# Output projection's tiles at other slots, and its reciprocal root on another engine, in an attention layer with a feed-forward layer

## What is computed

```python
x = x + layernorm(attention(layernorm(x), Wqvk, Wo))   # 16 heads of 32, causal, softmax, then @ Wo
x = x + layernorm(ffn(layernorm(x), W1, b1, ..., W2, b2))
```

```python
wv = jnp.einsum('bsth,bthi->bshi', weights, v).reshape(b, s, d)
return wv @ Wo
```

## Time and profile before

| | us |
|---|---|
| median of 3 runs | 3446.77 (3444.99 to 3449.8) |
| profiled execution | 3445.31 |
| its span | 3443.5 |
| PE busy in the span | 3148.3 (91%) |
| DVE busy | 2237.1 (65%) |
| ACT busy | 2070.4 (60%) |
| POOL busy | 1327.9 (39%) |

### The profile page before, as it was taken

How to read it: one execution, slowest core, us unless ns; L and a number is a source line. 1 busy time by engine, 2 the same in 40 slices (tenths; PEclk the granted TensorE clock), 3 DMA queues, 4 the chain that set the end, 5 groups by cost and what they waited for, 6 DMA issues and landing times. The chain is left out here.

```text
span 3443.5 us, 76542 instructions
## 1 busy us (share of the span) xinstructions
PE 3148.3 (91%) x29476; PEld 1797.2 (52%) x29476; DVE 2237.1 (65%) x4207; ACT 2070.4 (60%) x2451; POOL 1327.9 (39%) x718
## 2 busy tenths in 40 slices
PE   7999898999898989989899858999999999999998
PEld 3444344766666666767676623444444444444443
DVE  5455555777676777767677624666666666666665
ACT  3222332988888887979797924555555555555554
POOL 2000000988888897979798930000000000000000
PEclk9999999999999999999999978999999999999999
DMA  6578783122222222222222132111111111111110
GB/s 181 171 218 248 232 260 90 52 70 82 58 84 64 81 69 78 63 84 58 86 66 79 44 101 90 37 38 39 37 37 37 37 37 37 37 37 37 37 37 25
DMA packets 328304, 279.95 MB, mean 81 GB/s; under 512 B 151056, under 2 KB 270032, under 8 KB 325968
## 3 DMA queue, kind: packets, MB, share of 16 engines
q1 hardware_dynamic: 328016, 275.82, 27.8%
HBM read 148.87 MB, written 92.80 MB: 70 GB/s over the span
## 5 line engine op out<-in xcount | busy, mean ns | idle before, releaser
L1257 POOL TENSOR_TENSOR a_prob_lo<-a_prob,a_prob_hi 128x2048 f16<-128x2048 f32 (+2 forms) x448 | 1191.9, 2689 | 185.8 <-ACT a_prob_hi L1168 184.2
L229 DVE TENSOR_REDUCE u_mx<-a_pw 128x4 f32<-128x512 f32 (+1 forms) x1178 | 730.6, 657 | 166.4 <-PE a_pw L215 126.6
L1158 ACT ACTIVATE a_prob<-a_pst,a_lift,w_exp_scale 128x1024 f32<-128x1024 f32 (+1 forms) x640 | 709.6, 1124 | 207.5 <-PE a_pst L1095 101.4
L1592 PE MATMUL f_ph<-f_xT,f_w 128*128 128x512 f16 x3072 | 707.5, 380 | 26.9 <-DMA f_xT<-f_xh 26.9
L1602 PE MATMUL f_py<-f_w,f_act 128*128 128x512 f16 x3072 | 707.6, 380 | 25.0 <-DVE f_work L1445 12.3
L1168 ACT ACTIVATE a_prob_hi<-a_prob 128x2048 f16<-128x2048 f32 (+2 forms) x448 | 583.3, 1302 | 0.0
L1559 ACT ACTIVATE f_hidden_work<-f_ph,w_turn,w_fold 128x512 f32<-128x512 f32 x256 | 199.3, 779 | 582.8 <-PE f_ph L1592 582.3
L1403 POOL TENSOR_TENSOR f_ve<-f_mv,f_eps 128x4 f32<-128x4 f32 x32 | 9.0, 283 | 1329.9 <-DVE f_mv L1427 1329.9
L1122 PE MATMUL a_acc<-u_vt,a_prob_hi 128*128 128x33 f16 x9216 | 466.0, 178 | 49.8 <-POOL a_prob_lo L1257 28.7
L1592 PEld LDWEIGHTS f_ph<-f_xT,f_w 128*128 128x128 f16 x3072 | 301.3, 98 | 392.2 <-issue 31.8
L1602 PEld LDWEIGHTS f_py<-f_w,f_act 128*128 128x128 f16 x3072 | 299.0, 98 | 395.4 <-issue 17.7
(11 more groups left out here) (161 smaller groups left out, 3345.7 us busy)
## 6 DMA issues: line engine op xcount, KB each, us to landing
qk_parts<-q_stage SPq DMA_DIRECT2D x128, 256.0 KB, 2.9
u_qp<-qk_parts SPq DMA_DIRECT2D x192, 128.0 KB, 2.7
u_kp<-qk_parts SPq DMA_DIRECT2D x192, 128.0 KB, 2.8
v_parts<-q_vstage SPq DMA_DIRECT2D x16, 1056.0 KB, 5.2
u_vt<-v_parts SPq DMA_DIRECT2D x32, 528.0 KB, 4.8
q_x<-in_L_attn_h_dram SPq DMA_DIRECT2D x16, 1024.0 KB, 8.6
q_raw<-in_L_ffn_W_dram SPq DMA_DIRECT2D x16, 1024.0 KB, 7.7
u_xr<-in_L_attn_h_dram SPq DMA_DIRECT2D x64, 256.0 KB, 3.1
```

The source lines that it names most:

```text
L229: dve.tensor_reduce(out, src[:, 0:n * len(heads)].rearrange("p (h n) -> p h n", n=n), AX_X, ALU.max).then_inc(units.released, 1)
L1158: act.activation(prob[:, k % PR, :, off:QC], pst[:, k % 2, :, off:QC], ACT.Exp, scale=exp_scale, bias=lift[:, :]).then_inc(exp_done, 1)
L1257: pool.tensor_tensor(prob_lo[:, first % HR:first % HR + steps, :, off:QC], prob[:, first % PR:first % PR + steps, :, off:QC], prob_hi[:, f ...
L1592: last = pe.matmul(ph[:, f % HB, :], w1s[:, a, k, f * P:(f + 1) * P], xT[:, e, b, k, :], start=(j == 0), stop=(j == len(terms) - 1))
```

## The change

The tiles of a set begin at slots 10, 18, 26, ... 66, counted from the batch's last unit: 10 and 18 of unit 3, 6 and 14 of the next unit 0, 2, 10 and 18 of unit 1, 6 of unit 2. Since the last tiles now read group 0 after the next batch has begun to write it, `oT` gets a fifth place, and group 0 uses the one or the other in turn. For this the place must be known by batch parity, so the loop of six turns of one batch becomes one of three turns of two batches.

The reciprocal root moves from POOL's two instructions to eight of DVE with 128x1 elements: an approximation from the bits, then two polynomial steps. Each waits for the one before. Step 0 stands at the end of slot s + 2, step 1 at the start of s + 3, step 2 at the end of s + 3, and so on to step 7 at the start of s + 6; the start is before the slot's shared items and `normalise`, the end behind them. The output is written at s + 6 and stored at s + 7. The last batch's tiles do all eight steps right behind the statistics and write at s + 3.

```diff
-WO_AT = list(range(10, 10 + 5 * QT, 5))
+WO_AT = list(range(10, 10 + 8 * QT, 8))
 WO_AT_LAST = WO_AT
-WO_STATS, WO_SMALL, WO_OUT, WO_STORE = 2, 2, 4, 5
+WO_STATS, WO_OUT, WO_STORE = 2, 6, 7
+LAST_OUT, LAST_STORE = 3, 4
+ROOT_STEPS = 8
+ROOT_AT = {(2, 1): (0,), (3, 0): (1,), (3, 1): (2,), (4, 0): (3,), (4, 1): (4,), (5, 0): (5,), (5, 1): (6,), (6, 0): (7,)}
...
+    def last_batch(self, b):
+        return (b == 0 and self.this and not self.after) or not self.this
...
-        oT = sb("oT", [P, 2, GROUPS, SEQ], F16)
+        oT = sb("oT", [P, 2, GROUPS + 1, SEQ], F16)
...
+            def turned_group(g, batch_parity):
+                return GROUPS if g == 0 and batch_parity else g
+
             def run_all(engine, run):
-                run(0, FIRST)
-                with engine.Fori(1, BATCH - 1) as i:
-                    run(i, MIDDLE)
-                run(BATCH - 1, LAST)
-                run(BATCH, DRAIN)
+                run(0, FIRST, 0)
+                with engine.Fori(0, BATCH // 2 - 1) as pair:
+                    run(2 * pair + 1, MIDDLE, 1)
+                    run(2 * pair + 2, MIDDLE, 0)
+                run(BATCH - 1, LAST, 1)
+                run(BATCH, DRAIN, 0)
...
+                def wo_root(i, t, step):
+                    n = QT * i + t
+                    v, y0, h0, y1, h1, slope, bow, y = (root[:, t % YR, c:c + 1] for c in range(ROOT_STEPS))
+                    g2 = ROOT_GAIN * ROOT_GAIN
+                    if step == 0:
+                        dve.wait_ge(mv_done, n + 1)
+                        dve.tensor_tensor(v, mv[:, t % YR, 1:2], eps, ALU.add).then_inc(root_step, 1)
+                        return
+                    dve.wait_ge(root_step, ROOT_STEPS * n + step)
+                    if step == 1:
+                        dve.tensor_scalar(y0.bitcast(I32), v.bitcast(I32), -0.5, float(ROOT_BITS), ALU.mult, ALU.add
+                                          ).then_inc(root_step, 1)
+                    elif step == 2:
+                        dve.scalar_tensor_tensor(h0, y0, v, y0, ALU.mult, ALU.mult).then_inc(root_step, 1)
...
                 def wo_out(i, t):
-                    dve.wait_ge(small_done, 2 * n + 2)
+                    dve.wait_ge(root_step, ROOT_STEPS * (n + 1))
...
-                def wo_small(i, t):
-
-                    n, s = QT * i + t, t % YR
-                    pool.wait_ge(mv_done, n + 1)
-                    pool.tensor_tensor(small[:, s, 0:1], mv[:, s, 1:2], eps, ALU.add).then_inc(small_done, 1)
-                    pool.wait_ge(small_done, 2 * n + 1)
-                    pool.tensor_tensor(small[:, s, 1:2], small[:, s, 0:1], half[:, :], ALU.pow).then_inc(small_done, 1)
```

More of the change, by code:

```diff
@@ L135 @@
 K_FREE_AT = max(k for k, (_c, j) in enumerate(STEPS) if j < TPC) + 1
-WO_AT = list(range(10, 10 + 5 * QT, 5))
+WO_AT = list(range(10, 10 + 8 * QT, 8))
 WO_AT_LAST = WO_AT
-WO_STATS, WO_SMALL, WO_OUT, WO_STORE = 2, 2, 4, 5
-assert all(TURN_AT[t // TQ] < at < NS + TURN_AT[t // TQ] for t, at in enumerate(WO_AT))
-TAIL = WO_AT_LAST[-1] + WO_STORE + 1 - NS
+WO_STATS, WO_OUT, WO_STORE = 2, 6, 7
+LAST_OUT, LAST_STORE = 3, 4
+ROOT_STEPS = 8
+ROOT_AT = {(2, 1): (0,), (3, 0): (1,), (3, 1): (2,), (4, 0): (3,), (4, 1): (4,), (5, 0): (5,), (5, 1): (6,), (6, 0): (7,)}
+ROOT_BITS, ROOT_NEAR, ROOT_GAIN = 0x5F1FFFF9, 2.38924456, 0.703952253
+assert all(TURN_AT[t // TQ] < at < 2 * NS + TURN_AT[t // TQ] for t, at in enumerate(WO_AT))
+TAIL = WO_AT_LAST[-1] + LAST_STORE + 1 - NS
 assert sum(PIECES_AT.values()) == len(PIECES)
@@ L943, in attention_phase @@
     LIFT = 8 * math.log(2)
-    CONST = 2
+    CONST = 1
     ctx = ExitStack()
@@ L969, in attention_phase @@
         mv = sb("mv", [P, YR, 2])
-        small = sb("small", [P, YR, 2])
-        half = sb("half", [P, 1])
+        root = sb("root", [P, YR, ROOT_STEPS])
         y = sb("y", [P, YR, D])
@@ L1014, in _, with run @@
                 x1_v = x1.rearrange("b (t p) d -> b t p d", p=P)
-                def run(i, stage):
+                def run(i, stage, parity):
                     for u, k in stage.slots:
@@ L1032, in run @@
                             load_qk(sp, units, qk_parts, i, u + 2, 0, False)
-                        for b, t in stage.tiles(u, k, WO_STORE):
+                        stored = [(b, t) for b, t in stage.tiles(u, k, WO_STORE) if not stage.last_batch(b)]
+                        stored += [(b, t) for b, t in stage.tiles(u, k, LAST_STORE) if stage.last_batch(b)]
+                        for b, t in stored:
                             sp.wait_ge(y_done, QT * (i + b) + t + 1)
@@ L1069, in shared, with project @@
                     last.then_inc(work_done, 1)
-                def project(i, before, b, t, g, stage):
+                def project(i, before, b, t, g, stage, parity):
                     n = QT * (i + b) + t
@@ L1078, in project @@
                         pe.wait_ge(released, before + turn + 1)
+                    held = turned_group(g, (parity + b) % 2)
                     for w, a in PASSES:
-                        last = pe.matmul(pwo[:, :], oT[:, a, g, t * P:(t + 1) * P], wo[:, w, g, :],
+                        last = pe.matmul(pwo[:, :], oT[:, a, held, t * P:(t + 1) * P], wo[:, w, g, :],
                                          start=(g == 0 and (w, a) == PASSES[0]),
@@ L1147, in run @@
                                 for g in range(2 * part, 2 * part + 2):
-                                    project(i, before, b, t, g, stage)
+                                    project(i, before, b, t, g, stage, parity)
                 run_all(pe, run)
@@ L1201, in normalise, with turned @@
                                       ).then_inc(o_done, 1)
-                def turned(i, u, c, at, before, bank):
-                    cols = slice(c * QC, (c + 1) * QC)
+                def turned(i, u, c, at, before, bank, parity):
+                    cols, held = slice(c * QC, (c + 1) * QC), turned_group(u % UNITS, parity)
                     dve.wait_ge(work_done, before + at + 1)
-                    dve.tensor_copy(oT[:, 0, u % UNITS, cols], pw[:, bank, 0:QC]).then_inc(oT_hi, 1)
+                    dve.tensor_copy(oT[:, 0, held, cols], pw[:, bank, 0:QC]).then_inc(oT_hi, 1)
                     dve.wait_ge(oT_hi, NC * (UNITS * i + u) + c + 1)
-                    dve.tensor_tensor(oT[:, 1, u % UNITS, cols], pw[:, bank, 0:QC],
-                                      oT[:, 0, u % UNITS, cols], ALU.subtract).then_inc(released, 1)
+                    dve.tensor_tensor(oT[:, 1, held, cols], pw[:, bank, 0:QC],
+                                      oT[:, 0, held, cols], ALU.subtract).then_inc(released, 1)
                 def wo_stats(i, t):
@@ L1217, in wo_stats @@
                     dve.bn_aggr(mv[:, s, :], stats[:, s, :]).then_inc(mv_done, 1)
+                def wo_root(i, t, step):
[12 more added lines that the diff above has]
+                        dve.scalar_tensor_tensor(h0, y0, v, y0, ALU.mult, ALU.mult).then_inc(root_step, 1)
+                    elif step == 3:
+                        dve.scalar_tensor_tensor(y1, h0, -ROOT_NEAR, y0, ALU.add, ALU.mult).then_inc(root_step, 1)
+                    elif step == 4:
+                        dve.scalar_tensor_tensor(h1, y1, v, y1, ALU.mult, ALU.mult).then_inc(root_step, 1)
+                    elif step == 5:
+                        dve.tensor_scalar(slope, h1, -ROOT_GAIN * g2 * g2 * 3 / 8, ROOT_GAIN * g2 * 10 / 8, ALU.mult,
+                                          ALU.add).then_inc(root_step, 1)
+                    elif step == 6:
+                        dve.tensor_tensor(bow, slope, h1, ALU.mult).then_inc(root_step, 1)
+                    else:
+                        dve.scalar_tensor_tensor(y, bow, -ROOT_GAIN * 15 / 8, y1, ALU.add, ALU.mult
+                                                 ).then_inc(root_step, 1)
@@ L1225, in wo_out, with roots @@
                                              ALU.add).then_inc(y_done, 1)
-                def shared(i, at, before, what, unit, m, stage):
+                def roots(i, stage, u, k, late):
+                    for (lag, end), steps in ROOT_AT.items():
+                        for b, t in stage.tiles(u, k, lag):
+                            if end == late and not stage.last_batch(b):
+                                for step in steps:
+                                    wo_root(i + b, t, step)
@@ L1228, in shared, with run @@
+                def shared(i, at, before, what, unit, m, stage, parity):
                     bank = (work_before(0, stage) + at) % 2
                     if what == "turn":
-                        turned(i, unit, m, at, before, bank)
+                        turned(i, unit, m, at, before, bank, parity)
                     else:
                         maxima(i, at, before, what, unit, m, bank)
-                def run(i, stage):
+                def run(i, stage, parity):
                     before = work_before(i, stage)
@@ L1238, in run @@
```

(17 more changed lines are left out.)

4 lines of the change are left out of this document (2 added, 2 removed).

## The result

The change makes the kernel slower: 3734.3 us at the median of four runs (3710.6 to 3750.2), against 3447.7 us (3445.0 to 3449.8) for four runs of the kernel before. The ratio is 1.083 (95% interval 1.077 to 1.089), so 287 us were added where 28 fewer were forecast. The profiled execution of after is the longest of its runs, 3750.2 us.

What follows compares the result with a forecast made beforehand. ACT and POOL were taken to bound units without tiles. Loop -21, sets -11, last batch's unit 3 -4.1 and drain +7.9 gave -28 us, from 3446.8 to 3418 us; range 3388 to 3445.

Steps and rivals of the forecast that it cites:

- Root on DVE: Attention phase, eight 128x1 root steps a tile on DVE: 3.7 us a set charged, bounds 0 and 10.6.
- Two of its own signs of being wrong: More PE waits for `u_mx` at root steps, unit 2 above 44 us, ACT waits over 2 us behind slot 18.
- Loop of pairs: Attention phase's batch loop: two jumps back in place of five, 7.0 us each, 21 us less (18 to 23).
- New slots: Attention phase, a set's eight tiles at their new slots, priced without the root: 17.2 us a set.
- Last batch's unit 3: Last batch's unit 3: ACT's 4.11 us stall goes, 4.1 us less, the unit near 37 us.
- Drain: From the last exponentials to the last output: 50.2 us in place of 42.3, 7.9 us more (4 to 11).
- slower, by the roots: Rival, DVE's slots 0 to 15: every step costs its whole 0.19 us, 10.6 a set, 3466 us; chance 0.11.
- More distance alone buys nothing; other slots do: Attention phase: waits end right behind each tile, before the next five slots on, so only other slots help.
- all hidden: Rival, tiles spread over 64 slots: PE's debt is paid back between tiles, 14 us a set, 3370 to 3385; chance 0.12.
- The bounds: Cost of a set of eight tiles: terms' bounds give 14 to 33 us; half way to each, 17 and 25.

Runs made afterwards that it cites:

- control: Kernel before with plain copies in place of the 128 DMAs that turn the normalised x, attention phase untouched: 3440.4 us, later 3441.5 us.

## Why the prediction was wrong

**The step that failed is "Root on DVE".** It took 0.19 us for each of the eight instructions, from rows that lie outside the attention phase or whose instructions read one tensor, and put the bounds at nothing and at 8 x 0.19. Nothing in it asked what a DVE instruction that reads two SBUF tensors does while POOL reads SBUF. In the trace of before no small instruction of that kind stands in the attention phase; `wo_out` reads PSUM and SBUF and was never long (741 to 752 ns). The price of a step is 0.15 to 0.22 us, or the rest of the POOL instruction then running, up to 4.0 us. POOL is busy for 37 of every 38 us in an empty unit, and six of eight steps are exposed. The rule cited above would have decided it, and the prediction didn't weigh it. Two of its own signs of being wrong came: PE's waits for `u_mx` on the score pieces rose from 31.5 to 152.1 us, and unit 2 took 51.5 us where it had put the line at 44.

By terms. Against a control of 3441.5 the whole change costs 272.7 us: the loop, the order and the drain with the root on POOL give -29.7 (that kernel against its control), eight single-tensor steps on DVE in place of POOL's root +22.6, and the second tensor in six of them +279.8. The last is measured by the kernel without it; the excess of the long steps gives 252 of it. The other 28 us aren't attributed: the mean granted clock over the span is 0.928 with the second tensor and 0.978 without, and which part of the 28 is the clock's no run separates. Without the blocking, with single-tensor steps, the change gains 7 us on its control, where 28 were forecast.

- *Loop of pairs*, -21 (18 to 23): measured -24.9. The mechanism was right, and so was the count of waits. A jump is worth more than its two waits: they fell by 30.5 - 11.5 = 19.0 us, the time by 24.9. The unit behind a jump also shows a lower granted clock (0.91 to 0.94), but its part isn't separated, and the control's own runs spread over 6 us.
- *New slots*, 17.2 a set without the root: with POOL's root and what is left of its waits a set costs 21.3 in place of 22.5, so slots and later output together are worth some 1 us, not 5. How that splits between slot 18, slot 2 and POOL's wait wasn't measured.
- *Root on DVE*, 3.7 a set (0 to 10.6): the whole set, forecast at 20.9, takes 69.9 us in the batch shown, and with 21.3 for it with POOL's root, the roots make 48.6 of that. On average over the sets, (287 + 25 - 7 - 12) / 7 = 42 us above the 22.5 of before, so 64: the loop's 25 us are added, and the last unit's 7.0 and the drain's 12.2 taken away. Without the second tensor a set costs 23.5, some 2.2 more than with POOL's root.
- *Last batch's unit 3*, 37.1: 48.2 in after; 39.0 with the root on POOL and 38.1 with single-tensor steps. That ACT's stall of 4.1 us behind POOL goes was right: ACT waits for POOL in none of the three. But it goes with the root on POOL too, so by the slots and not by the move of the root; and in after ACT stands 11.1 us for PE in its place.
- *Drain*, 50.2: 54.5 in after (2296.0 to 2350.5), 57.6 with single-tensor steps, 51.1 with the root on POOL, where the order of the tiles and an earlier output slot are what differs from before. So the moved tiles cost 8.8 where 7.9 - 3.9 = 4.0 was forecast; the steps cost 54.5 - 51.1 = 3.4 in after, near the 3.9 forecast, and 6.5 as single-tensor steps.
- *The rival "slower, by the roots"* named the right place, with a chance of 0.11, but a wrong mechanism and a price of 0.19 us a step; it gave 3466. Single-tensor steps land at 3434, not there: they cost 2.2 us a set more than POOL's root with its waits, not 10.6.
- "*More distance alone buys nothing; other slots do*" holds. Tiles at slots 10 and 17 of every unit cost 12.0 us a set. So the 14 us a set of the rival *all hidden* can be had, but by the choice of slots and not by spreading the tiles.
- *The bounds.* Half way from 20.9 to the upper 33 a set is 27, not 25. With 27 the upper end of the range is 3464, still 270 us under what was measured.

## What to carry to other kernels

Before moving a small operation to DVE, look at what POOL does in that stretch: if it is reading SBUF, a DVE instruction with two SBUF tensors can cost what is left of POOL's instruction, however few elements it has (up to 4.0 us for one column here, and more in the case below), and the queue behind it pays too. Give it one tensor and per-partition scalars, let one input come from PSUM, or leave it on POOL and let its reader come later. When the mean of a group is far from what its shape suggests, look at shortest, median and longest, and then at what the neighbour was doing at the start and the end of one long instance.

## What was unexpected of the hardware

With POOL's instructions halved, one step was blocked far beyond the instruction it had met, where the rule cited above ends the blocking with that instruction. DVE's timeline, then POOL's (one row for twelve instructions without a gap):

```profile
2154.80 18.68 DVE L1244 TENSOR_TENSOR a_root<-a_mv,w_wo_eps 128x1 f32<-128x1 f32 x1
```

```profile
2153.22 20.24 POOL L1323 TENSOR_TENSOR a_prob_lo<-a_prob,a_prob_hi 128x1024 f16<-128x1024 f32 x12
```

The step began while the first of the twelve was running and ended at 2173.48 us, 0.02 after the last. In that kernel seven more, all on L1251, waited for one POOL instruction beyond the one they had met (0.70 to 0.75 us in all), and in the kernel with one two-tensor step there is one such case (2.14 us). Those eight had begun within some 0.1 us of the end of the instruction that they met. All the other long steps ended with the one they had met. Why one was passed over by eleven stays open; that POOL never paused is what the rows show. Smaller POOL instructions are therefore no sure cure.

Second, a scalar per partition isn't free. With one in place of an immediate or a second tensor, a 128x1 step takes 0.20 to 0.21 us, with two 0.26 to 0.27, against 0.154 with immediates alone.
